# Layer 2's scores computed for two heads at once, each in its own row half of the array

## The reference

```python
q = jnp.einsum('bsd,hpd->bhsp', x, q_w) + q_b
k = jnp.einsum('bsd,hpd->bhsp', x, k_w) + k_b
v = jnp.einsum('bsd,hpd->bhsp', x, v_w) + v_b
scores = jnp.einsum('bhqp,bhkp->bhqk', q, k) / jnp.sqrt(jnp.float32(P))
attn = jax.nn.softmax(scores, axis=2)          # over the queries
ctx = jnp.einsum('bhqk,bhkp->bqhp', attn, v)
out = concat @ l_w.T + l_b                     # concat: ctx of all 16 heads
```

## Time and profile before

| what | value |
|---|---|
| median of 3 executions | 1751.83 us (1751.59 to 1757.77) |
| the profiled execution | 1753.32 us, of which the span on the engines is 1751.5 us |
| mean granted TensorE clock, whole span | 0.941 |
| PE, DVE, ACT, POOL busy over the span | 86%, 76%, 59%, 20% |
| layer 2's attention, first qk to last ctx | 696.5 to about 1414 us |

### The profile page before, as it was taken

One profiled execution on the slowest core, in us unless ns is written; L12 is line 12 of the kernel. 1 busy time (PEld: TensorE's weight loads), 2 busy tenths in 40 slices (PEclk: granted clock), 3 DMA queues, 4 the chain that ended last, 5 costly groups with the idle time before them and its releaser, 6 DMA issues.

```text
span 1751.5 us, 22707 instructions
## 1 busy us (share of the span) xinstructions
PE 1503.8 (86%) x7723; PEld 705.8 (40%) x7723; DVE 1329.5 (76%) x2839; ACT 1028.6 (59%) x1897; POOL 349.0 (20%) x334
## 2 busy tenths in 40 slices
PE   6668988988867778899999999999899989786666
PEld 3522222222257466343434343334344334454645
DVE  7765566664457676888888888887888849998997
ACT  4358788778643122667676766667667765461232
POOL 3000000000012331101111112111111114443654
PEclk9789999999988978999999999999999989898887
DMA  3245555444200100434333333333333400000001
GB/s 85 33 125 126 127 125 132 126 124 129 87 5 1 62 1 1 88 74 134 72 73 73 72 73 73 72 71 69 85 70 76 97 1 1 1 1 0 7 13 30
DMA packets 85619, 114.48 MB, mean 65 GB/s; under 512 B 13568, under 2 KB 50688, under 8 KB 85120
## 3 DMA queue, kind: packets, MB, share of 16 engines
q1 hardware_dynamic: 85504, 113.04, 26.7%
HBM read 54.27 MB, written 7.34 MB: 35 GB/s over the span
## 4 chain that ended last, share of the span: by engine, by line
PE 46%; DVE 31%; ACT 13%; issue 7%; POOL 1%; DMA 1%; SPq 1%; ACTq 0%; DVEq 0%; POOLq 0%
PE ps L1944 10%; PE ps L1933 8%; PE ps L546 7%; PE ps L255 6%; ACT p4E L2032 5%; DVE p4mx L1988 4%; DVE p6ac L2501 3%; DVE WA L2535 3%; DVE xn L171 2%; PE ps L1922 2%; DVE p4T L1972 2%; ACT p1g L264 2%; PE ps L1911 2%; PE ps L554 1%; PE ps L686 1%
## 5 line engine op out<-in xcount | busy, mean ns | idle before, releaser
L2032 ACT ACTIVATE p4E<-ps,p4mx,p4sc 128x512 f32<-128x512 f32 x512 | 391.6, 776 | 200.8 <-DVE p4mx L1990 198.3
L1988 DVE TENSOR_REDUCE p4mx<-ps 128x2 f32<-128x1024 f32 x256 | 311.8, 1218 | 31.4 <-PE ps L1933 31.4
L1933 PE MATMUL ps<-p4Q,p4K 128*128 128x512 f16 x1024 | 260.1, 381 | 20.5 <-ACT p4E L2032 14.9
L1944 PE MATMUL ps<-p4E,p4vn 128*64 128x512 f32 x1024 | 265.0, 609 | 5.9 <-POOL p4vn L2051 4.4
L581 DVE SCALAR_TENSOR_TENSOR p1Pb<-ps,WB,p1sh 128x512 f32<-128x512 f32 x128 | 96.0, 750 | 131.4 <-PE ps L546 127.1
L2051 POOL TENSOR_TENSOR p4vn<-p4v,p4zs 128x256 f32<-128x256 f32 x128 | 78.6, 614 | 578.5 <-DVE p4zs L1994 578.5
L255 PE MATMUL ps<-p1R,p1w1s 128*128 128x512 bf16 x512 | 151.4, 393 | 36.3 <-ACT p1g L264 21.1
L1933 PEld LDWEIGHTS ps<-p4Q,p4K 128*128 128x128 f16 x1024 | 84.9, 97 | 228.1 <-ACT p4E L2032 88.7
L165 POOL TENSOR_TENSOR rs<-rs,cst 128x4 f32<-128x4 f32 x58 | 60.8, 1048 | 532.7 <-DVE rs L159 532.7
L264 ACT ACTIVATE p1g<-ps,WB 128x1024 f32<-128x1024 f32 x128 | 136.5, 1113 | 43.7 <-PE ps L255 43.6
L546 PE MATMUL ps<-p1g,WB 128*32 128x512 f32 x512 | 138.3, 629 | 0.0
(11 more groups left out here) (358 smaller groups left out, 2702.4 us busy)
## 6 DMA issues: line engine op xcount, KB each, us to landing
p1sh<-gscr SPq DMA_DIRECT2D x128, 256.0 KB
p4K<-p4T SPq DMA_DIRECT2D x256, 128.0 KB, 2.4
p4Q<-p4T SPq DMA_DIRECT2D x256, 64.0 KB, 2.1
p1R<-tscr SPq DMA_DIRECT2D x64, 128.0 KB, 5.2
tscr<-p1tp SPq DMA_DIRECT2D x24, 128.0 KB, 1.7
WA<-in_w SPq DMA_DIRECT2D x1, 2632.0 KB, 9.4
WB<-in_w SPq DMA_DIRECT2D x1, 2560.0 KB, 10.4
X<-in_x SPq DMA_DIRECT2D x8, 256.0 KB, 6.0
```

The source lines that it names most:

```text
L1933: t = p.e.matmul(ps[:, at + a, :], self.KK[i][:, hh, part, 128 * j:128 * j + 128], self.QQ[i][:, hh, :], start=part == 0, stop=part == 1)
L1944: t = p.e.matmul(ps[64 * hh:64 * hh + 64, 7, :], vn[u % 4][:, j, :], E[u % 4][:, j, :], start=j == 0, stop=j == 3)
L1988: v.e.tensor_reduce(m, ps[:, at:at + 2, :], AX, ALU.max).then_inc(v.own.h, v.one())
L2032: a.e.activation(self.E[u % 4][:, j, :], ps[:, at + i, :], ACT.Exp, bias=self.mx[u % 4][:, j:j + 1], scale=pre.sc[:, 1, 0:1], accum_out=se ...
```

## The change

- The tiles K and Q and their 8 DMAs for each pair go; SP has nothing to issue at `qk`.
- A score step is now (n, j): one key block of both heads. PE makes six matmuls that contract 64 rows: three products (K high x Q high, K low x Q high, K high x Q low), each for head 0 in rows 0 to 63 and right behind it for head 1 in rows 64 to 127. Head 0 writes the first bank of the bank pair, head 1 the second. They read T itself.
- The order of PE within a pair becomes: score, score, ctx half 0, score, score, ctx half 1, project, and so on.
- `values` is one step for a pair, behind its last exponential: one reciprocal of 128x8 and one POOL multiplication of 128x512. The tiles mx, zs and vn are regrouped accordingly.
- Writing T(n + 2) waits for the scores of pair n where it waited for DMAs.

The core of the diff (the tiles' new shapes and the new counts in the waits of `vproj` are left out):

```diff
@@ order
-            if now:
-                yield "score", (n, 0, 0)
-                yield "score", (n, 0, 1)
-            if last:
-                yield "ctx", (n - 1, 0)
-            if now:
-                yield "score", (n, 1, 0)
-                yield "values", (n, 0)
-            if last:
-                yield "ctx", (n - 1, 1)
-            if now:
-                yield "score", (n, 1, 1)
+            for j in range(4):
+                if now:
+                    yield "score", (n, j)
+                if j % 2 and last:
+                    yield "ctx", (n - 1, j // 2)
             if last:
                 yield "ctx out", n - 1
...
             if now:
-                yield "values", (n, 1)
+                yield "values", n
             if n + 2 < 64:
                 yield "qk", n + 2
@@ released
         if what == "score":
-            p.wait_ge(k.sem("E"), 4 * (2 * x[0] + x[1]) + 2 * x[2] + 2)
+            p.wait_ge(k.sem("E"), 8 * x[0] + 2 * x[1] + 2)
@@ tensor
             elif what == "score":
-                n, hh, c = x
-                i, at = n % 2, self.bank["score", x]
+                n, j = x
+                t, at = self.T[n % 2], self.bank["score", x]
                 self.released(p, ("score", x))
-                p.wait_ge(k.sem("kq", i), 128 * (n // 2 + 1))
-                for a in range(2):
-                    j = 2 * c + a
-                    for part in range(2):
-                        t = p.e.matmul(ps[:, at + a, :], self.KK[i][:, hh, part, 128 * j:128 * j + 128], self.QQ[i][:, hh, :],
-                                       start=part == 0, stop=part == 1)
-                t.then_inc(k.sem("score").h, 1)
+                p.wait_ge(k.sem("thi"), 2 * n + 2)
+                p.wait_ge(k.sem("tlo"), 2 * n + 2)
+                for o, (q, r) in enumerate(self.PARTS):
+                    for hh, rows in enumerate((slice(0, 64), slice(64, 128))):
+                        y = p.e.matmul(ps[:, at + hh, :], t[rows, q, 128 * j:128 * j + 128], t[rows, 2 + r, :], start=o == 0, stop=o == 2)
+                y.then_inc(k.sem("score").h, 1)
@@ vector, scalar
-                v.wait_ge(k.sem("kq", x % 2), 128 * (x // 2))
+                v.wait_ge(k.sem("score"), 4 * x - 4)
...
-                a.wait_ge(k.sem("kq", x % 2), 128 * (x // 2))
+                a.wait_ge(k.sem("score"), 4 * x - 4)
...
-                v.wait_ge(k.sem("E"), 4 * u + 4)
-                v.e.reciprocal(zs[u % 4][:, :], zs[u % 4][:, :]).then_inc(k.sem("zr").h, 1)
+                v.wait_ge(k.sem("E"), 8 * x + 8)
+                v.e.reciprocal(zs[x % 2][:, :, :], zs[x % 2][:, :, :]).then_inc(k.sem("zr").h, 1)
@@ gpsimd
-                g.e.tensor_tensor(self.vn[u % 4][:, :, :], self.vv[b % 2][:, :, 64 * h:64 * h + 64],
-                                  self.zs[u % 4][:, :].unsqueeze(2).to_broadcast([128, 4, 64]), ALU.mult).then_inc(k.sem("vn").h, 1)
+                two = lambda t: t.rearrange("p a (b c) -> p a b c", b=2)
+                g.e.tensor_tensor(two(self.vn[x % 2][:, :, :]), two(self.vv[b % 2][:, :, 128 * hp:128 * hp + 128]),
+                                  self.zs[x % 2][:, :, :].unsqueeze(3).to_broadcast([128, 4, 2, 64]), ALU.mult).then_inc(k.sem("vn").h, 1)
@@ sync
-            if what == "qk":
-                i, T, KK, QQ = x % 2, self.T[x % 2], self.KK[x % 2], self.QQ[x % 2]
-                sp.wait_ge(k.sem("tlo"), 2 * x + 1)
-                sp.wait_ge(k.sem("score"), 4 * (x - 2) + 4)
-                for hh in range(2):
-                    r = slice(64 * hh, 64 * hh + 64)
-                    for d in (slice(0, 64), slice(64, 128)):
-                        sp.e.dma_start(KK[d, hh, :, :], T[r, 0:2, :]).then_inc(k.sem("kq", i).h, 16)
-                sp.wait_ge(k.sem("tlo"), 2 * x + 2)
-                for hh in range(2):
-                    r = slice(64 * hh, 64 * hh + 64)
-                    for a, d in enumerate((slice(0, 64), slice(64, 128))):
-                        sp.e.dma_start(QQ[d, hh, :], T[r, 2 + a, :]).then_inc(k.sem("kq", i).h, 16)
```

More of the change, by code:

```diff
@@ L66 @@
     "gu": ("uvar", 9), "ht": ("urstd", 9), "y7": ("us2", 34), "w_5": ("x_in_0", 16), "w_6": ("x_in_1", 16),
[1 row of a table removed]
+    "up5": ("x_in_2", 16), "out": ("x_in_3", 16),
 }
@@ L1806, in __init__ @@
         self.T = [loc(f"T{i}", [128, 4, 512], F16) for i in range(2)]
-        self.KK = [loc(f"K{i}", [128, 2, 2, 512], F16) for i in range(2)]
-        self.QQ = [loc(f"Q{i}", [128, 2, 512], F16) for i in range(2)]
         self.vv = [loc(f"v{i}", [128, 4, 1024]) for i in range(2)]
         self.E = [loc(f"E{i}", [128, 4, 512]) for i in range(4)]
-        self.mx = [loc(f"mx{i}", [128, 4]) for i in range(4)]
-        self.zs = [loc(f"zs{i}", [128, 4]) for i in range(4)]
-        self.vn = [loc(f"vn{i}", [128, 4, 64]) for i in range(4)]
+        self.mx = [loc(f"mx{i}", [128, 4, 2]) for i in range(2)]
+        self.zs = [loc(f"zs{i}", [128, 4, 2]) for i in range(2)]
+        self.vn = [loc(f"vn{i}", [128, 4, 128]) for i in range(2)]
         self.cx = [loc(f"cx{i}", [128, 512]) for i in range(2)]
@@ L1938, in tensor @@
                 p.wait_ge(k.sem("cx"), n)
+                p.wait_ge(k.sem("vn"), n + 1)
+                p.wait_ge(k.sem("E"), 8 * n + 8)
                 for j in (2 * half, 2 * half + 1):
                     for hh in range(2):
-                        u = 2 * n + hh
-                        p.wait_ge(k.sem("vn"), u + 1)
-                        p.wait_ge(k.sem("E"), 4 * u + 4)
-                        t = p.e.matmul(ps[64 * hh:64 * hh + 64, 7, :], vn[u % 4][:, j, :], E[u % 4][:, j, :], start=j == 0, stop=j == 3)
+                        t = p.e.matmul(ps[64 * hh:64 * hh + 64, 7, :], vn[n % 2][:, j, 64 * hh:64 * hh + 64], E[2 * (n % 2) + hh][:, j, :],
+                                       start=j == 0, stop=j == 3)
                 if half:
@@ L1982, in vector @@
             elif what == "score":
-                n, hh, c = x
-                u, at = 2 * n + hh, self.bank["score", x]
-                m = mx[u % 4][:, 2 * c:2 * c + 2]
-                v.wait_ge(k.sem("score"), 2 * u + c + 1)
-                v.wait_ge(k.sem("E"), 4 * (u - 4) + 4)
+                n, j = x
+                at, m = self.bank["score", x], mx[n % 2][:, j, :]
+                v.wait_ge(k.sem("score"), 4 * n + j + 1)
+                v.wait_ge(k.sem("E"), 8 * n - 8)
                 v.e.tensor_reduce(m, ps[:, at:at + 2, :], AX, ALU.max).then_inc(v.own.h, v.one())
@@ L2024, in scalar @@
             elif what == "score":
-                n, hh, c = x
-                u, at = 2 * n + hh, self.bank["score", x]
-                a.wait_ge(k.sem("mx"), 2 * u + c + 1)
+                n, j = x
+                i, at = n % 2, self.bank["score", x]
+                a.wait_ge(k.sem("mx"), 4 * n + j + 1)
                 a.wait_ge(k.sem("ctx"), n - 1)
-                a.wait_ge(k.sem("vn"), u - 3)
-                for i in range(2):
-                    j = 2 * c + i
-                    a.e.activation(self.E[u % 4][:, j, :], ps[:, at + i, :], ACT.Exp, bias=self.mx[u % 4][:, j:j + 1], scale=pre.sc[:, 1, 0:1],
-                                   accum_out=self.zs[u % 4][:, j:j + 1]).then_inc(k.sem("E").h, 1)
+                a.wait_ge(k.sem("vn"), n - 1)
+                for hh in range(2):
+                    a.e.activation(self.E[2 * i + hh][:, j, :], ps[:, at + hh, :], ACT.Exp, bias=self.mx[i][:, j, hh:hh + 1], scale=pre.sc[:, 1, 0:1],
+                                   accum_out=self.zs[i][:, j, hh:hh + 1]).then_inc(k.sem("E").h, 1)
             elif what == "turn":
@@ L2065, in sync @@
         for what, x in self.order():
-            if what == "qk":
-                i, T, KK, QQ = x % 2, self.T[x % 2], self.KK[x % 2], self.QQ[x % 2]
-                sp.wait_ge(k.sem("tlo"), 2 * x + 1)
-                sp.wait_ge(k.sem("score"), 4 * (x - 2) + 4)
-                for hh in range(2):
-                    r = slice(64 * hh, 64 * hh + 64)
-                    for d in (slice(0, 64), slice(64, 128)):
-                        sp.e.dma_start(KK[d, hh, :, :], T[r, 0:2, :]).then_inc(k.sem("kq", i).h, 16)
-                sp.wait_ge(k.sem("tlo"), 2 * x + 2)
-                for hh in range(2):
-                    r = slice(64 * hh, 64 * hh + 64)
-                    for a, d in enumerate((slice(0, 64), slice(64, 128))):
-                        sp.e.dma_start(QQ[d, hh, :], T[r, 2 + a, :]).then_inc(k.sem("kq", i).h, 16)
-            elif what == "load":
+            if what == "load":
                 if x == 6:
```

11 lines of the change are left out of this document (4 added, 7 removed), and 1 row of the table AGAIN.

## The result

After the change the kernel takes 1759.7 us (median of 15, 1756.93 to 1768.4) against 1752.09 before (median of 15): 1.0043 times as long, with an interval of 1.0028 to 1.0058. So it is slower by 7.6 us, 0.43%, just under the half per cent that I had set as the border of no change. The forecast was 1761, range 1738 to 1784; its largest chance, 0.59, was on slower by more than 0.5%, and 0.26 on the case that came. The profiled execution took 1762.53, with a span of 1760.7, 9.2 above the span before.

The account below looks back on a forecast made before the run. Bound: a wait loop from the first two exponentials through PE's fourth score to the next pair's exponentials. 8.8 + 2 - 1.05 + 0.6 - 1 = +9.4 on the median 1751.8 gives 1761, range 1738 to 1784.

Parts of the forecast that it names:

- the case that came: Whole kernel about the same, within 0.5% (8.8 us), the border of no change; chance 0.26.
- The loop: Wait chain through PE's fourth score: plain pair 10.37, one vproj 11.66, two 12.95; +8.8 over 4 batches; chance 0.50.
- S: Time of a new score of six 64-row matmuls on PE: taken as 0.70, between bounds of 0.65 and 1.30.
- S near 0.9: Score time at which PE's own sum of work was said to meet the loop's period.
- no overlap: Rival: the row halves of PE's scores do not overlap, score time 1.30, whole kernel 1830; chance 0.08.
- Overlap with loss: Rival: each slot of two score matmuls also bears a 0.098 weight load, score time 0.94, kernel 1776; chance 0.18.
- The cover of `values`: POOL's one multiplication, up to 1.27, just hidden before the next pair's first ctx half; exposed once at stage end, +0.6.
- The second half: Pairs 32 to 61: up to 54 unchanged within 6 us, then seven plain pairs at +0.4; +2 in all.
- The small parts: DMAs gone -1.05 at the start, `values` exposed at the stage's end +0.6, last two pairs about -1.
- The clock: Rival: PE's pause and half-filled array bring granted clock 0.5 into the stage; +20 to +30, 1776; chance 0.06.
- my signs of being wrong: New score of 0.9 or more, granted clock below 1.00 between 706 and 1411, or pairs under 10.
- Faster: Rival: PE's relief counts and the wait before the fourth score does not; 1708, or 1735 at half; chance 0.13.

Follow-up runs that it names:

- the order alone: Kernel before the change with only its fourth score moved in front of ctx half 1: 1773.97 us, ratio 1.0132.
- both bounds lifted: Changed kernel with ctx half 1 back in front of the fourth score and `values` in two steps by key blocks: 1702.71 us, ratio 0.9712.
- one row half: Changed kernel with all six matmuls of a score on rows 0 to 63, head 0 in head 1's place: 1828.85 us in one execution.
- the order undone: Changed kernel with only ctx half 1 moved back in front of the fourth score: 1750.52 us, ratio 1.0003 to the kernel before.
- head by head: Changed kernel with a score's matmuls issued as three of head 0, then three of head 1: 1757.74 us, ratio 1.0043.
- the versions with the copies: Changed kernel with the 8 DMAs a pair kept, into tiles nobody reads: 1761.58 us; the second version, without DVE's wait for them, 1762.05 us.

## Why the prediction was right

**The loop (right).** Terms forecast and measured in pair 19: wait for two exponentials 1.68, 1.68; score and its switch 0.80, 0.75; ctx half 1.87, 1.87; project 0.89, 1.00; vproj 1.29, 1.29; qk to the next first exponential 5.13, 5.06. Three of them were off by -0.05, +0.11 and -0.07; these cancel, so the periods came out within 0.02: 10.35, 10.79, 11.65 and, over pairs 20 and 21, 24.59, against 10.37, 10.81, 11.66 and 24.61. The batch gained 2.07 where +2.2 was forecast. The first half as a whole came to +7.5, not 4 x 2.2 = 8.8, because the first batch gained only 1.3: pair 0 has no ctx and pair 1 no project on the loop, and both ran at ACT's pace (9.64 and 9.63). That the order makes this and not the scores' price is shown from both sides: the order alone slowed the old kernel, and undone it freed the new one. The project term was read from a place where a full-array score stood in front of it; behind ctx it costs 0.11 more, in the kernel after as with the order alone, and behind a score on row halves 0.10 more (884.23 to 885.22, both bounds lifted). The Trainium skill's page TensorEngine Tiling (Array Packing), section Key Properties, says that a switch of mode drains the array, which would explain it; it gives no time, and the 0.11 here agrees with the 0.10 into ctx.

**S (right, at its lower bound).** On the loop the score takes 0.65 and its switch 0.10, against 0.70 and 0.10; the 0.05 that I added for the loads is not there. Two in a row take 1.48 with the switch behind them, 0.08 more than twice 0.65 and a switch of 0.10 would give. "S near 0.9", the point from which I let "no overlap" decide, does not follow from my own sums: PE's sum in a plain pair is 6.15 + 4 S and the loop 9.67 + S, and they meet at S = 1.17. Of the rivals, "no overlap" had its mechanism and price right and its condition wrong: with one row half it came out at 1828.85 for a forecast 1830. "Overlap with loss" has no row for it: even three matmuls in a row on the same half are as fast.

**The cover of `values` (mis-sized, without cost in the steady pairs).** I put its start at 6.4 after the pair's first exponential and its length at up to 1.27: just hidden. It begins at 7.40 (893.79 to 901.19) and takes 1.04, since it needs all eight exponentials and DVE's reciprocal; so it ends at 8.4, and PE, which reaches ctx at 901.95, waits 0.43. After, POOL and then PE:

```profile
901.19 1.04 POOL L2038 TENSOR_TENSOR p4vn<-p4v,p4zs 128x512 f32<-128x512 f32 x1 [9.27 <-DVE p4zs L1983]
```

```profile
902.38 1.94 PE L1934 MATMUL ps<-p4E,p4vn 128*64 128x512 f32 x8 [0.43 <-POOL p4vn L2038]
```

The prediction said that a lost cover would go to the fourth score's slack first, and it did. At the stage's end it was not covered: I put +0.6 there, and PE's last ctx waited 2.56 (1418.51). What I did not see is that it stands as the next bound right behind the loop. The same error is in my expectation for the order undone, which lies 30 us or more below what came: the wait for vn is missing there too.

**The second half (right in sign, partly by luck).** +3.4 for +2. Two falls of the clock, which my sum puts at nothing, make 3.2 of it; head by head, where they did not come, the second half takes 338.71, +0.5. The eight periods from pair 54 on gave +1.8 for the forecast +2. The part that I left at "unchanged, within 6" gave +1.6, and has gains and losses. One loss is the pair from 45 to 46, 14.44 after and 12.76 before. DVE, after:

```profile
1215.28 2.58 DVE L1971 SCALAR_TENSOR_TENSOR p4v<-ps,p4sc,WA 128x1024 f32<-128x1024 f32 x2 [1.68 <-PE ps L1914]
1217.77 2.33 DVE L1713 SCALAR_TENSOR_TENSOR p5up<-WB,p5nb,p5up 64x2048 f16<-64x2048 f32 x1
```

vproj comes late on PE, its two evacuations come late on DVE, and the next layer's long step stands between them and the reciprocal and the low part of T. How the other pairs add up I did not take apart. That the span's +9.2 came so near the +9.4 is luck in part: the first half was 1.3 below its forecast and the second 1.4 above.

**The small parts.** DVE's first maximum has no wait in front of it any more, as forecast. That the stage starts 0.95 earlier, for a forecast 1.05, does not show it: with the order alone, which keeps the copies and this wait of 1.05, it starts 3.3 earlier. The last pairs' tail and the vn exposed there were put at -1 and +0.6; what lies behind pair 62 came to -0.8. The DMAs cost nothing in the steady state, which the versions with the copies show.

**The clock (the rival happened, small).** A granted clock below 1.00 between 706 and 1411 was one of my signs of being wrong, and it came: 0.99 from 1060 on. In the steady batch it stayed at 1.00, also with half-filled matmuls (in every kernel here). It fell behind PE's longest waits, which the change brought: 2.23 in front of a fourth score, 2.15 in front of ctx. Priced at +20 to +30 for a tenth of the stage, it held for 10 us of 705 and cost about 3. The mechanism of the rival was there, its size was not.

**Faster.** This rival needed PE to reach the fourth score more than 1.68 after the first exponential. PE came early instead. In pair 20, without a wait for vn, it has the third score behind it 5.39 after qk's start and the first exponential comes at 5.06, so 1.35 are left to wait for the forecast 1.45; the profile shows 1.18, because it counts from the shown end of the matmuls. Where a wait for vn lies in front, less is left: 1.01 in pair 19 and 0.71 in pair 17. Its price was well sized: with both bounds lifted, which is another kernel, the time is 1702.71, near its 1708.

## What to carry to other kernels

In a queue that works in order, a step that waits for a buffer belongs behind work that is ready. Before you move such a step, add up the chain from the release that it waits for back to the same release one round later; if that sum is above the busiest engine's work, relief of that engine is worth only what of it lies on the chain (here one score of four). When you free a loop, name the next wait as well: two edits worth 11.3 and 2.5 us of the stage alone were worth 55.9 together. Read the granted clock over the whole stage, not over one batch: where it falls behind a wait, the wait costs more than itself. A step merged to save instructions (one multiplication in place of two) starts only when its last input is there, and its first reader pays for that.

## What the runs showed of the hardware

- Matmuls that contract 64 rows in different row halves overlap in whatever order they are issued: 12 of 512 columns in 1.48 with the halves alternating, 1.47 with three of one half in a row, 2.69 all on one half, each time with the switch into ctx. The Trainium skill (TensorE: Matmul & The Clock Gate, section Part 3: Packing small matmuls — row/col tiling) has row tiles start about 4 ns apart; the trace agrees, with the two matmuls of a pair starting within 0.01 of each other and the pairs 0.22 apart, and no run here shows what reorders or buffers the ones issued head by head.
- Project's eight matmuls take 0.89 behind full-array ones, 1.00 behind column-half ones and 0.99 behind row-half ones. A ctx half starts 0.10 later behind a score than the score's own rate gives.
- The granted clock fell to its lower level behind waits of PE of 2.0 to 2.6 us (2.23 and 2.15 in the kernel after, 2.57 and 2.03 with the order undone), but not each time: head by head the same 2.23 passed without a fall. A ctx half of 1.94 took 3.53 at the lower level.
- One more wait instruction in DVE's queue, for copies that had been issued two pairs earlier, cost 0.07 in front of an instruction that was waiting for ACT.
- POOL's multiplication of 128x512 took 1.04 and of 128x256 0.61: one large one is 0.18 less work than two small ones, and was still the worse choice.
